# Reordered steps in two attentions, and another order of the opening in a feed-forward with ternary weights

## The chip, the cores and the metric

The kernel runs on one core of one Trainium2 chip. Its time is the device time of the program in microseconds (us). All times of the trace come from one profiled execution and count from its first instruction. The engines are PE (TensorE, matrix products; its weight loads, PEld, run beside it), DVE (VectorE), ACT (ScalarE), POOL (GpSimd) and SP (SyncE, which here only issues transfers). Each engine runs its own list of instructions in order; an instruction waits on semaphores that others raise.

## What is computed

Four layers follow each other on 16 blocks x[b] of 128 rows and 256 columns: L0 to L3, each an attention (L0a, L1a, L2a, L3a) and a feed-forward (L0f, L1f, L2f, L3f; L3f is itself an attention with weights mixed from experts). The change touches L1a, L1f and L3f:

```
# L1a: 16 heads of 16 columns; v's rows are dropped where the column sums of the probabilities are least
scores = softmax(q @ k.T / 4);  keep = int(S * 0.9)
mask = 1 for the `keep` keys with the largest scores.sum(over queries)
x = x + concat((scores * mask) @ v) @ Wo.T + bo
# L1f: two linear layers, weights rounded to -1, 0, 1, inputs to 8 bits
def bitlinear(x, w, b):
    x = x * rsqrt(mean(x * x) + 1e-5)
    s = 127 / max(abs(x), per row);  xq = round(x * s) / s
    return xq @ (round(w / mean(abs(w))) * mean(abs(w))).T + b
x = x + bitlinear(gelu(bitlinear(layernorm(x), w1, b1)), w2, b2)
# L3f: per block, Wq, Wk, Wv are a weighted sum of two of four experts
Wc = sum(weights[b, e] * W[e]);  x = x + softmax(q @ k.T / 4) @ v @ Wo + bo
```

## The kernel before

Everything stays on the chip: x_all holds the 16 blocks, each section (L1a, L1f, ...) is a stretch of its own with a barrier at either end, and each engine's list is written out by hand. An attention goes through the blocks one per turn (`step`). The names `cur`, `prev`, `nxt`, `new` stand for the block of the turn, the one before it and the next two; `last` is two blocks back in L1a (kind PRUNED) and one in L3f (kind MIXED). A block has its 16 heads in four quarters j of four heads.

In a turn PE computes the scores of `cur` (four banks S), turns the probabilities of each quarter (`turn_probs`, banks T[0] and T[1] in turn; a bank is free once the quarter two before was copied out), multiplies `last` with its values, turns the reciprocals of its row sums (`turn_recips`), projects k, q and v of `nxt` through one bank F, and `project_out`s `last`. ACT takes the exponentials (four instructions a quarter, line 900) and copies the turned reciprocals (rT, line 928); the turned quarters are copied out by ACT in L1a (line 548), by DVE and ACT in L3f (`mine`, lines 550 and 548). DVE takes the row minima (line 989), adds the biases of k, q and v (lines 1003, 1009, 1023), writes the normalised output oT (`norm_out`, line 1071) for which `project_out` (line 771) waits, and adds the result to x_all (`add_out`, line 1077). In L1a it also finds the keys to drop. In L3f ACT and DVE mix the weights of `new` in two parts each (`mixing.share`, `mixing.more`, lines 2562 and 2569); the first share waits for the v bias of a block two before.

L1f works on pairs of blocks, s = 0 and 1, in eight turns. Its opening turns the rounded weights on PE in ten lots (four of w1, two of the bias rows, four of w2; line 2015) and copies them to bf16 on ACT (line 1849). DVE aggregates the statistics (line 1902), POOL raises to the power -1/2 in two lots, of the first two blocks and of the other 14 (line 1727; once for the layer norm, once for the scale). For a pair DVE then normalises (xn, line 194), takes the row maxima (line 1928), the factor and the inverse (line 1942), ACT scales and rounds (xs, line 1882), PE turns it (line 2048) and ACT copies it out (xqT, line 1889). POOL splits the inverse in bf16 parts (lines 1816 to 1820), which PE turns (line 2032) for the bias product (line 2055) ahead of the w1 products (line 2057). ACT takes the GELU (line 1872), DVE its row maxima (line 1958) and rounds (hs, line 1981), PE turns it back (line 2025, banks T2), ACT and DVE copy (lines 1854 and 1962), PE multiplies with w2 (line 2039), DVE adds to x_all (line 1950), ACT sums squares (line 1862), and POOL adds the bias b2 (`add_b2`, line 1800). In a turn `old` is finished, `cur` is between the layers, `nxt` enters, and on DVE `far` is prepared. Turns 2 to 7 run in a counted loop.

Of the kernel before, what the change touches and what calls it, by code (L numbers as in the profile page):

```python
# [453 lines left out]
def attention(nc, g, name, kind, w, turned, needs, later=(), beside=None, after=None, out=None):  # L454
# [5 lines left out]
    with sec:  # L460
# [91 lines left out]
        with sec.block() as block:  # L552
# [96 lines left out]
            def _(pe):  # L649
# [141 lines left out]
                def step(st):  # L791
# [6 lines left out]
                    if pruned:  # L798
# [7 lines left out]
                        piece(nxt, project_k, new, prev)  # L806
                        piece(last, project_out)
                        piece(cur, turn_probs, 1)
# [81 lines left out]
            def _(act):  # L890
# [89 lines left out]
                if kind not in (MIXED, PLAIN):  # L980
                    load_table(act, g, ACT.Sqrt)

            @block.vector
            def _(dve):
# [102 lines left out]
                def step(st):  # L1087
# [43 lines left out]
                    else:  # L1131
# [28 lines left out]
                        mine(cur, 0)  # L1160
                        piece(last, norm_out)
# [569 lines left out]
def bitlinear_ffn(nc, g, w, q3, bias):  # L1731
# [4 lines left out]
    with sec:  # L1736
# [34 lines left out]
        flat = T2[0] + T2[1] + H[0] + H[1]  # L1771
# [9 lines left out]
        s_t_ps, s_t_sb = sec.sem("turned_ps"), sec.sem("turned_sb")  # L1781
        SPLIT = 5
        with sec.block() as block:
            @block.gpsimd
            def _(pool):
                pool.memset(a6[:, :], 0.0).then_inc(s_split, 1)
                for n, (lo, hi) in enumerate(((0, NS), (NS, NB))):
                    pool.wait_ge(ln.s_aggr, n + 1)
                    root_ln.pool(pool, g, ln.rstd[:, lo:hi, 0], base[:, lo:hi], ln.mv[:, lo:hi, 1], 1.0, LN_EPS, n + 1)
                    pool.wait_ge(s_ms, 2 * n + 2)  # L1790
                    if n == 0:
                        pool.wait_ge(root_ln.s, 1)
                    root_x.pool(pool, g, root[:, lo:hi], base[:, lo:hi], ms[:, lo:hi], 1.0, 1e-5, n + 1)
                pool.wait_ge(s_w2, 1)
# [40 lines left out]

                for n in range(TURNS + 2):
                    if n >= 2:
                        dequant(Pair(NS * (n - 2), n - 1))
                    if n < TURNS:
                        split(Pair(NS * n, n + 1))  # L1840
                        add_b2(Pair(NS * n, n + 1))

            @block.scalar
            def _(act):
                act.activation(warm[:, :], g.eps[:, :], ACT.Gelu)
                for k in range(len(lots)):
                    act.wait_ge(s_t_ps, k + 1)
                    sources, dst = lots[k]
                    act.copy(dst, flat[k % 8][:, :].bitcast(BF16)[:, 0:len(sources) * P]
                             .rearrange("p (m n) -> p m n", m=len(sources))).then_inc(s_t_sb, 1)  # L1850

                def turn_back(q, s, m):
                    act.wait_ge(s_qT_ps[1][s], q.v)
                    return act.activation(hqT[s][:, 4 * m:4 * m + 4, :],
                                          T2[s][m][:, :].rearrange("p (c t) -> p c t", c=4),
# [8 lines left out]
                def step(old, cur, nxt):  # L1864
# [1185 lines left out]
```

## Time and profile before

| | us |
|---|---|
| median of 3 runs | 1147.53 (1144.92 to 1149.98) |
| the profiled execution | 1141.54 |
| its span, first to last instruction | 1139.7 |

| engine | busy us | share of the span | instructions |
|---|---|---|---|
| PE | 1000.3 | 88% | 9262 |
| PEld | 815.5 | 72% | 9262 |
| DVE | 872.6 | 77% | 2482 |
| ACT | 724.1 | 64% | 2778 |
| POOL | 286.7 | 25% | 527 |

The mean granted clock of PE is 0.953 of full speed. The shares are means over sections with different limits, so the change has to be read section by section: L1a lies at about 240 to 420, L1f at 420 to 510 and L3f at 960 to 1140.

### The profile page before, as it was taken

The page shows a single profiled execution, that of the slowest core. Times are in us where ns is not written, and L with a number is a line of the kernel's source. Part 1 is how long each engine was busy: PE and PEld are TensorE (multiplying, and loading weights), DVE is VectorE, ACT ScalarE, POOL GpSimd, SP SyncE. Part 2 cuts the span into 40 slices and gives each one's busy share as a digit, 9 for nine tenths or more (in the row PEclk, how much of TensorE's full clock was granted, in tenths as well). Part 3 has the DMA queues.
Part 4 walks back from the last instruction along what each step waited for, and adds up shares of the span by engine and source line. Part 5 has one row for each costly group of instructions (what it writes and reads, how often), then busy time and mean ns, then how long its engine had stood idle before and what let it go on. Part 6 is the DMA issues. An engine that isn't in the chain of part 4 may idle for free. (4 is left out here: it accounts for less than half of the span.)

```text
span 1139.7 us, 27783 instructions
## 1 busy us (share of the span) xinstructions
PE 1000.3 (88%) x9262; PEld 815.5 (72%) x9262; DVE 872.6 (77%) x2482; ACT 724.1 (64%) x2778; POOL 286.7 (25%) x527
## 2 busy tenths in 40 slices
PE   6999967669999967878999979999997997889997
PEld 4888853247777843557777758999996986667775
DVE  5888989877888856975777755566655798689996
ACT  4887876768888866975777763112112544589995
POOL 4454530012222234422222210000000131333331
PEclk9999999679999997998999989999999998799999
DMA  9510000000000000005221000000000010000000
GB/s 282 133 30 1 3 1 1 0 15 16 15 12 11 11 2 1 0 6 130 85 82 52 10 2 1 0 0 0 0 1 19 24 29 6 5 12 14 14 14 20
DMA packets 43285, 30.17 MB, mean 26 GB/s; under 512 B 17208, under 2 KB 42432, under 8 KB 43200
## 3 DMA queue, kind: packets, MB, share of 16 engines
q1 hardware_dynamic: 43200, 29.10, 9.0%
q8 instruction: 46, 0.75, 0.3%
q14 instruction: 39, 0.32, 0.1%
HBM read 22.80 MB, written 2.10 MB: 22 GB/s over the span
## 5 line engine op out<-in xcount | busy, mean ns | idle before, releaser
L900 ACT ACTIVATE L1a_pr<-L1a_scores,L1a_nm 128x128 f32<-128x128 f32 x256 | 92.8, 415 | 4.5 <-DVE L1a_nm L989 3.8
L900 ACT ACTIVATE L2a_pr<-L2a_scores,L2a_nm 128x128 f32<-128x128 f32 x256 | 90.6, 390 | 6.0 <-DVE L2a_nm L989 6.0
L900 ACT ACTIVATE L0a_pr<-L0a_scores,L0a_nm 128x128 f32<-128x128 f32 x256 | 90.7, 395 | 4.4 <-DVE L0a_nm L989 4.4
L900 ACT ACTIVATION_READ_ACCUMULATOR L1a_pr<-L1a_scores,L1a_nm 128x1 f32 x256 | 65.1, 254 | 0.0
L989 DVE TENSOR_REDUCE L2a_nm<-L2a_scores 128x4 f32<-128x512 f32 x64 | 42.2, 683 | 24.9 <-PE L2a_scores L718 24.9
L2195 PE MATMUL L2f_inner<-L2f_taT,L2f_loraBT 128*128 128x128 f32 x512 | 59.7, 275 | 0.9 <-DVE L2f_hs L2347 0.9
L900 ACT ACTIVATION_READ_ACCUMULATOR L0a_pr<-L0a_scores,L0a_nm 128x1 f32 x256 | 60.1, 235 | 0.0
L2267 ACT COPY L2f_xTb<-L2f_xT 128x256 f32<-128x256 f32 x16 | 6.3, 411 | 84.5 <-PE L2f_inner L2184 84.5
L2184 PEld LDWEIGHTS L2f_inner<-L2f_xTb,L2f_wiT 128*128 128x128 f32 x512 | 58.3, 192 | 1.5 <-ACT L2f_loraBT L2151 1.2
L2184 PE MATMUL L2f_inner<-L2f_xTb,L2f_wiT 128*128 128x128 f32 x512 | 58.6, 275 | 0.9 <-ACT L2f_loraBT L2151 0.9
L2195 PEld LDWEIGHTS L2f_inner<-L2f_taT,L2f_loraBT 128*128 128x128 f32 x512 | 58.4, 192 | 1.1 <-issue 1.1
L900 ACT ACTIVATION_READ_ACCUMULATOR L2a_pr<-L2a_scores,L2a_nm 128x1 f32 x256 | 58.6, 229 | 0.0
L2208 PE MATMUL L2f_y_ps<-L2f_woT,L2f_hs 128*128 128x256 f32 x256 | 57.6, 379 | 0.0
L2208 PEld LDWEIGHTS L2f_y_ps<-L2f_woT,L2f_hs 128*128 128x128 f32 x256 | 47.6, 190 | 5.9
L2427 POOL MEMSET early_gates_spread_r<- 128x256 f32 x1 | 0.3, 312 | 198.2 <-POOLq L75 198.2
L900 ACT ACTIVATE L3f_pr<-L3a_logits_ps,L3f_nm 128x128 f32<-128x128 f32 x128 | 45.0, 382 | 3.6 <-DVE L3f_nm L989 3.6
L989 DVE TENSOR_REDUCE L1a_nm<-L1a_scores 128x4 f32<-128x512 f32 x64 | 41.0, 683 | 5.5 <-PE L1a_scores L718 5.1
L2562 ACT ACTIVATE mixing_mix<-experts,gates 128x1028 f32 (+1 forms) x32 | 33.5, 1046 | 18.1 <-DVE L3f_v L1023 14.1
L900 ACT ACTIVATE L3f_pr<-L3a_h_tilde,L3f_nm 128x128 f32<-128x128 f32 x128 | 44.8, 380 | 0.0
L671 PE MATMUL L3a_turned<-L3f_xT,mixing_mix 128*128 128x128 f32 x256 | 38.3, 296 | 7.3 <-ACT L3f_xT L907 6.8
L989 DVE TENSOR_REDUCE L0a_nm<-L0a_scores 128x4 f32<-128x512 f32 x64 | 42.0, 680 | 2.8 <-PE L0a_scores L718 2.8
L671 PEld LDWEIGHTS L3a_turned<-L3f_xT,mixing_mix 128*128 128x128 f32 x256 | 33.8, 205 | 11.8 <-ACT L3f_xT L907 10.3
(621 smaller groups left out, 3147.2 us busy)
## 6 DMA issues: line engine op xcount, KB each, us to landing
L_ffn_w_w<-in_L_ffn_w SPq DMA_DIRECT2D x2, 1024.0 KB, 6.8
L1a_ctxT<-ctxT_all SPq DMA_DIRECT2D x16, 128.0 KB, 2.0
L2a_ctxT<-ctxT_all SPq DMA_DIRECT2D x16, 128.0 KB, 2.0
L3a_mem<-in_ctx SPq DMA_DIRECT2D x16, 128.0 KB, 2.1
out<-x_all SPq DMA_DIRECT2D x16, 128.0 KB, 1.7
L0a_ctx_nat<-in_ctx SPq DMA_DIRECT2D x1, 1280.0 KB, 12.4
x_all<-in_x SPq DMA_DIRECT2D x1, 1024.0 KB, 9.4
L_ffn_wi<-in_L_ffn_wi SPq DMA_DIRECT2D x1, 1024.0 KB
```

The costliest lines, as they stand in the source:

```text
L671: mm = pe.matmul(F[:, m * P:m * P + P], W[:, c, m * P:m * P + P], inp[:, c, :], start=(c == 0), stop=(c == DC - 1))
L900: ex = act.activation(pr[q.s][:, j, h, :], S[j][:, h * P:h * P + P], ACT.Exp, bias=nm[q.s][:, j, h:h + 1], scale=-1.0, accum_out=ls[q.s][: ...
L989: dve.tensor_reduce(nm[q.s][:, j, :], S[j][:, :].rearrange("p (h k) -> p h k", h=2 * DC), AX.X, ALU.min).then_inc(s_mx[q.s], 1)
L2184: mm = pe.matmul(U[s][f // 4][:, f % 4 * P:f % 4 * P + P], wiT[:, c, f * P:f * P + P], xTb[s][:, c, :], start=(f % 4 == 0 and c == 0), sto ...
L2195: mm = pe.matmul(U[s][f // 4][:, f % 4 * P:f % 4 * P + P], bT[:, f * P:f * P + P], tb[s][:, k, :], start=False, stop=(k == 1), skip_group_ ...
L2208: mm = pe.matmul(Y[s][:, 0:D], hs[s][:, f, :], woT[:, f, :], start=(f == 0), stop=(f == FC - 1))
L2267: act.copy(xTb[s][:, :, :], xT[s][:, :, :]).then_inc(s_xTb[s], 1)
L2427: pool.memset(self.spread_r[:, :, :], 0.0).then_inc(self.s_set, 1)
L2562: act.activation(self.mix[q.s][:, lot], g.experts[:, first, lot], ACT.Copy, scale=g.gates[:, q.b, 0, :]).then_inc(self.s_share[n][q.s], 1)
```

## The change

Four edits. In L1a PE turns quarter 1 of `cur` ahead of `project_out` instead of behind it, and ACT's last instruction there loads the table of Gelu instead of that of Sqrt. In L3f DVE writes `norm_out` ahead of the copy of `cur`'s quarter 0. In L1f the opening has another order: the warm-up Gelu is gone; ACT copies w1 and the bias rows, scales the first pair, and only then copies two of the four w2 lots, while DVE copies the other two; POOL takes the powers of the 14 later blocks behind the first pair's split, and their second lot behind its add_b2; DVE aggregates those 14 behind the first pair's preparation. The banks of the lots follow from that (`turned_in`). Within the loop PE turns `nxt` between the two streams' second products instead of behind them. The last pair's turned h goes to the banks H, and its wait for the output of the pair before moves from the turning to the product.

```diff
@@ L1a, PE
                         piece(nxt, project_k, new, prev)
+                        piece(cur, turn_probs, 1)
                         piece(last, project_out)
-                        piece(cur, turn_probs, 1)
                         piece(nxt, project_q)
@@ attention, end of ACT's list
-                if kind not in (MIXED, PLAIN):
-                    load_table(act, g, ACT.Sqrt)
+                if kind in (PRUNED, MASKED):
+                    load_table(act, g, ACT.Gelu if pruned else ACT.Sqrt)
@@ L3f, DVE
-                        mine(cur, 0)
-                        piece(last, norm_out)
+                        if kind == MIXED:
+                            piece(last, norm_out)
+                            mine(cur, 0)
...
@@ L1f
-        flat = T2[0] + T2[1] + H[0] + H[1]
+        turned_in = T2[0] + T2[1] + [H[0][1], H[1][1]] + T2[0] + T2[1]
...
+        W1, B1 = range(4), range(4, 6)
+        W2_ACT, W2_DVE = range(6, 8), range(8, 10)
...
+        def turned(q):
+            return H if isinstance(q.v, int) and q.v == TURNS else T2
...
+                norm_roots(0, 0, NS)
+                scale_roots(0, 0, NS)
+                pool.wait_ge(s_w2, 1)
                 for n in range(TURNS + 2):
                     if n >= 2:
                         dequant(Pair(NS * (n - 2), n - 1))
                     if n < TURNS:
                         split(Pair(NS * n, n + 1))
+                        if n == 0:
+                            norm_roots(1, NS, NB)
                         add_b2(Pair(NS * n, n + 1))
+                        if n == 0:
+                            scale_roots(1, NS, NB)
@@ L1f, ACT
-                act.activation(warm[:, :], g.eps[:, :], ACT.Gelu)
-                for k in range(len(lots)):
...
+                take_weights(W1)
+                take_weights(B1)
...
+                    if nxt and not cur:
+                        take_weights(W2_ACT)
@@ L1f, DVE
                     if far:
+                        if nxt and not cur:
+                            mean_squares(1, NS, NB)
                         prepare(far, nxt)
                         if not nxt:
-                            mean_squares(1, NS, NB)
                             dve.wait_ge(root_x.s, 1)
                         if nxt and not cur:
                             dve.wait_ge(root_x.s, 2)
                         dequant(far, nxt)
+                        if not nxt:
+                            statistics(1, NS, NB)
+                            for k in W2_DVE:
+                                dve.wait_ge(s_t_ps, k + 1)
+                                dve.tensor_copy(*turned_lot(k)).then_inc(s_t_dve, 1)
...
-                statistics(1, NS, NB)
                 sweep_four(dve, step)
@@ L1f, PE
+                def turn_next(nxt, cur):
+                    for s in range(NS):
+                        pe.wait_ge(s_scaled[0][s], nxt.v)
...
                         for s in range(NS):
                             pe.wait_ge(s_scaled[1][s], old.v)
-                            pe.wait_ge(s_x[s], old.v)
+                            if turned(old) is T2:
+                                pe.wait_ge(s_x[s], old.v)
...
+                            if turned(old) is H:
+                                pe.wait_ge(s_x[s], old.v)
                             for f in range(FC):
                                 mm = pe.matmul(T2[s][0][:, 0:D], hqT[s][:, f, :], w2T[:, f, :], start=(f == 0),
                                                stop=(f == FC - 1))
                             mm.then_inc(s_y[s], 1)
+                            if s == 0 and nxt:
+                                turn_next(nxt, cur)
```

## Rows read from the trace of the kernel before

**Rows 1.** Windows of one turn: us, PE, PEld, DVE, ACT, POOL busy, clock, DMA share, GB/s.

```profile
320.25:330.27 10.02, 9.57 (x126) 7.92 (x125) 8.51 (x33) 8.27 (x38) 2.63 (x4) 1.00 0.04 13
...
440.84:451.77 10.93, 9.57 (x49) 5.68 (x50) 7.96 (x21) 8.03 (x16) 3.62 (x11) 0.75 0.01 2
...
478.19:487.11 8.92, 7.24 (x50) 4.89 (x50) 8.22 (x24) 8.15 (x16) 3.75 (x11) 1.00 0.00 0
```

**Rows 2.** Waits in L1a, 250 to 400: us in total, times, longest us.

```profile
PE L1a_values L771 <- DVE L1a_oT L1071: 5.4, 13, 0.5
```

**Rows 3.** Timeline of L1f's opening.

```profile
422.14 2.02 ACT L1849 COPY L1f_w1T<-L1f_h_turned 128x512 bf16<-128x512 bf16 x4
...
422.85 0.70 POOL L1727 TENSOR_TENSOR L1f_root<-L1f_base,minus_half 128x2 f32<-128x2 f32 x1
...
423.35 0.71 DVE L194 TENSOR_SCALAR L1f_xn<-x_all,L1f_ln_mv,L1f_ln_rstd 128x256 f32<-128x256 f32 x2
...
424.04 1.96 ACT L1849 COPY L1f_b1T<-L1f_hidden 128x1024 bf16<-128x1024 bf16 x2
...
427.31 2.58 POOL L1727 TENSOR_TENSOR L1f_root<-L1f_base,minus_half 128x14 f32<-128x14 f32 x1
...
427.75 1.18 ACT L1882 ACTIVATE L1f_xs<-L1f_xn,magic,L1f_factor 128x256 f32<-128x256 f32 x2
...
431.05 1.41 POOL L1800 TENSOR_TENSOR x_all<-x_all,L_ffn_b 128x256 f32<-128x256 f32 x2
...
431.25 0.26 PE L2032 MATMUL L1f_hidden<-identb,L1f_inverse_parts 128*128 128x128 bf16 x1 [7.60 <-POOL L1f_inverse_parts L1820]
...
431.69 1.24 DVE L194 TENSOR_SCALAR L1f_xn<-x_all,L1f_ln_mv,L1f_ln_rstd 128x256 f32<-128x256 f32 x2
...
432.59 0.58 PE L2055 MATMUL L1f_hidden<-L1f_b1T,L1f_inverse_rows 128*128 128x512 bf16 x1 [0.23 <-ACT L1f_xqT L1889]
...
434.23 0.16 DVE L1942 RECIPROCAL L1f_inverse<-L1f_dequant 128x2 f32<-128x2 f32 x1
...
436.65 1.22 DVE L1958 TENSOR_REDUCE L1f_am<-L1f_h 128x1 f32<-128x1024 f32 x1 [2.26 <-ACT L1f_h L1872]
```

**Rows 4.** Waits of DVE in L1f's loop, 452 to 497.

```profile
DVE L1f_am L1958 <- issue: 1.3, 4, 0.4
```

**Rows 5.** Timeline of a turn of L1a: start us, us, engine, line, what.

```profile
325.28 0.64 ACT L548 COPY L1a_prT<-L1a_probsT 128x512 f32<-128x512 f32 x1
...
326.23 1.13 PE L771 MATMUL L1a_values<-L1a_WoT,L1a_oT 128*128 128x256 f32 x4 [0.45 <-DVE L1a_oT L1071]
...
327.53 0.42 DVE L1077 TENSOR_TENSOR x_all<-L1a_values,x_all 128x256 f32 x1
...
327.64 1.06 PE L671 MATMUL L1a_projected<-L1a_xT,L1a_WqT 128*128 128x128 f32 x8
...
328.73 0.42 DVE L1009 TENSOR_TENSOR L1a_qT<-L1a_projected,L_xattn_bq 128x256 f32<-128x256 f32 x1 [0.19 <-PE L1a_projected L671]
```

**Rows 6.** Timeline of a turn of L1f's loop.

```profile
485.20 1.03 PE L2039 MATMUL L1f_h_turned<-L1f_w2T,L1f_hqT 128*128 128x256 bf16 x8 [0.60 <-DVE L1f_hqT L1962]
...
486.86 0.86 DVE L1950 SCALAR_TENSOR_TENSOR x_all<-L1f_h_turned,L1f_dequant,x_all 128x256 f32 x2
```

**Rows 7.** Timeline of L1f's last turn.

```profile
501.93 1.45 DVE L1981 TENSOR_SCALAR L1f_hs<-L1f_h,L1f_factor 128x1024 f32<-128x1024 f32 x2
...
503.92 1.94 PE L2025 MATMUL L1f_h_turned<-ident,L1f_hs 128*128 128x128 f32 x16 [1.01 <-DVE x_all L1950]
```

**Rows 8.** Waits of PE in L3f, 1010 to 1106.

```profile
PE L3a_turned L771 <- DVE L3f_oT L1071: 6.9, 10, 0.7
```

**Rows 9.** Timeline of a turn of L3f.

```profile
1056.90 1.03 PE L701 MATMUL L3a_turned<-mixing_mix,L3f_xT 128*128 128x256 f32 x4
...
1057.55 0.40 DVE L194 TENSOR_SCALAR L3f_xn<-x_all,kept_mv,kept_rstd 128x256 f32 x1
...
1057.97 0.42 DVE L1023 TENSOR_TENSOR L3f_v<-L3a_turned,mixing_mix 128x256 f32<-128x256 f32 x1
```

More of the change, by code:

```diff
@@ L1159, in step @@
                             late.vector_pooled(dve, T[1])
-                        mine(cur, 0)
-                        piece(last, norm_out)
+                        if kind == MIXED:
+                            piece(last, norm_out)
+                            mine(cur, 0)
+                        else:
+                            mine(cur, 0)
+                            piece(last, norm_out)
                         piece(nxt, add_q)
@@ L1961, in step @@
                         dve.wait_ge(s_qT_ps[1][1], old.v)
-                        dve.tensor_scalar(hqT[1][:, 4:8, :], T2[1][1][:, :].rearrange("p (c t) -> p c t", c=4),
+                        dve.tensor_scalar(hqT[1][:, 4:8, :], turned(old)[1][1][:, :].rearrange("p (c t) -> p c t", c=4),
                                           MAGIC, None, ALU.subtract).then_inc(s_qT2, 1)
@@ L2011, in _ @@
                         bias.wait(pe)
-                    if k >= 8:
-                        pe.wait_ge(s_t_sb, k - 7)
+                    if k >= 6:
+                        pe.wait_ge(s_t_sb, k - 5)
                     for m, src in enumerate(sources):
-                        mm = pe.transpose(flat[k % 8][:, :].bitcast(BF16)[:, m * P:m * P + P], src, g.identb[:, :])
+                        mm = pe.transpose(turned_in[k][:, :].bitcast(BF16)[:, m * P:m * P + P], src, g.identb[:, :])
                     mm.then_inc(s_t_ps, 1)
-                pe.wait_ge(s_t_sb, len(lots))
+                def turn_next(nxt, cur):
+                    for s in range(NS):
+                        pe.wait_ge(s_scaled[0][s], nxt.v)
+                        if cur:
+                            pe.wait_ge(s_gelu[s], cur.v)
+                        for c in range(DC):
+                            mm = pe.transpose(XT[s][:, c * P:c * P + P], xs[s][:, c * P:c * P + P], g.ident[:, :])
+                        mm.then_inc(s_qT_ps[0][s], 1)
                 def step(old, cur, nxt):
                     if old:
+                        if isinstance(old.v, int) and old.v == 1:
+                            pe.wait_ge(s_t_sb, W2_ACT[-1] + 1)
+                            pe.wait_ge(s_t_dve, len(W2_DVE))
                         for s in range(NS):
                             pe.wait_ge(s_scaled[1][s], old.v)
-                            pe.wait_ge(s_x[s], old.v)
+                            if turned(old) is T2:
+                                pe.wait_ge(s_x[s], old.v)
                             for f in range(FC):
-                                mm = pe.transpose(T2[s][f // 4][:, f % 4 * P:f % 4 * P + P],
+                                mm = pe.transpose(turned(old)[s][f // 4][:, f % 4 * P:f % 4 * P + P],
                                                   hs[s][:, f * P:f * P + P], g.ident[:, :])
                             mm.then_inc(s_qT_ps[1][s], 1)
+                    if nxt and not cur:
+                        turn_next(nxt, cur)
                     if nxt:
@@ L2031, in step @@
                             pe.wait_ge(s_gelu[0], cur.v)
+                        else:
+                            pe.wait_ge(s_t_sb, B1[-1] + 1)
                         pe.transpose(AT, a6[:, :], g.identb[:, :]).then_inc(s_aT_ps, 1)
@@ L2041, in step @@
                             mm.then_inc(s_y[s], 1)
+                            if s == 0 and nxt:
+                                turn_next(nxt, cur)
                     if nxt:
-                        for s in range(NS):
-                            pe.wait_ge(s_scaled[0][s], nxt.v)
-                            if cur:
-                                pe.wait_ge(s_gelu[s], cur.v)
-                            for c in range(DC):
-                                mm = pe.transpose(XT[s][:, c * P:c * P + P], xs[s][:, c * P:c * P + P], g.ident[:, :])
-                            mm.then_inc(s_qT_ps[0][s], 1)
+                        if cur and not old:
+                            turn_next(nxt, cur)
                         pe.wait_ge(s_aT, nxt.v)
```

23 lines of the change are left out of this document (13 added, 10 removed).

## The prediction

> **What bounds the kernel now.** I read the windows by turn first (where is an engine full?), then the waits of the engine that is full, then the timeline around each edited line, and asked there what ends last.
>
> In L1a a turn takes 10.02 us and PE is busy for 9.57 of it, DVE and ACT for under 8.6 [rows 1]: PE sets the pace, and the 0.45 it does not work is one wait, project_out for DVE's normalised output; it comes back in 13 turns with 5.4 us [rows 2]. With the first such turn, which lies outside that stretch's full turns, I count 14.
>
> In L1f two regimes follow each other. Its opening is a chain over four engines in which PE stands still for 7.60 us ahead of the first real work [rows 3]. From the third turn on the loop takes 8.92 us with DVE busy 8.22 and ACT 8.15 [rows 1]; DVE is the one that waits for nobody there (its only idle time before the big reduction is "issue", 1.3 us in four turns) [rows 4]. So the loop runs at DVE's pace, and what PE or ACT gains in it is worth nothing, but whatever the opening saves on DVE's clock is carried to the end. In L3f a turn is a ring through DVE, ACT and PE; DVE's last step of it, the v bias, starts right behind PE's v projection.
>
> **The change part by part.**
>
> *L1a, probabilities ahead of the output projection.* In the turn shown, project_out starts at 326.23 after a wait of 0.45, so PE was free at 325.78 [rows 5]. The step that now stands there, turn_probs(cur, 1), wants the exponentials of its quarter and a free T[1], which ACT's copy of the previous block's last quarter gives back at 325.28 + 0.64 = 325.92 [rows 5]. PE can go on at about 325.98, so 0.25 of the 0.45 is saved; project_out comes about 0.2 later than now. Nothing is added and no DMA moves: one queue (PE) is reordered, and the waits are those the two steps had. Who waits for project_out: DVE's add_out (327.53), behind which the statistics and the q bias are queued. A project_out that ends 0.1 to 0.2 later pushes add_out by about 0.08, since it now starts 0.17 after project_out's end. The q bias waits 0.19 for PE's project_q [rows 5], which comes 0.25 earlier; DVE's own queue allows at most those 0.19, less the 0.08. So 0.11 to 0.19 a turn; I take 0.13, times 14: **1.8 us**. Bounds: 0 (DVE's push eats it) and 14 x 0.19 = 2.7.
>
> *The table at L1a's end, and the warm-up.* The load at the end of L1a stays, of another table; L2a's is as before. L1f's opening loses a load and an activation ahead of ACT's first weight copy (422.14 [rows 3]). Worth about 1.0 on ACT (PE's first transposes bound it), counted in the next part.
>
> *L1f's opening, first pair.* Now: ACT copies ten lots, from 422.14 until xs begins at 427.75; POOL takes both long powers (14 columns, 2.58 us each) before it splits the first pair's inverse, so PE's turn of it is at 431.25 and the first hidden matmul at 432.59 [rows 3]. After: ACT has four lots (2.02) and two bias lots (1.96) before xs. From 422.14, xs is at 426.1; with the warm-up gone about 425.1. Then xs 1.18, two w2 copies (half of 2.02), and the xqT step: hidden matmuls at about 427.9, 4.7 earlier. POOL does not stand in the way any more: xn starts at about 422.5 (now 423.35, behind 14 aggregations), and from xn to the inverse the second pair took 431.69 to 434.39, of which 0.53 was xn being slow (1.24 against 0.71) [rows 3]; so the inverse is there at 422.5 + 2.2 = 424.7 and split, which now takes 429.89 to 431.25, is done at 426.1. The DVE takes two w2 copies here, an estimate of 0.6 each (half of a 1024-wide pass of 1.22 [rows 3]); they lie in time in which DVE has nothing else.
>
> *L1f's opening, second pair.* What was in front is now behind: the first long power runs 426.1 to about 429.0, add_b2 (1.41) to 430.4, the second long power to 433.3 (0.3 for the step ahead of each is an estimate). DVE's dequant of the second pair waits for it, and behind that wait in DVE's queue stands the big reduction of the first pair's GELU. So it starts at about 433.8, not at 436.65 [rows 3]: 2.9 earlier, although its input is ready before. Both reductions then run back to back (2 x 1.22), so the next hidden matmuls, now at 440.84 [rows 1], can start at about 436.8. I take **4.0 us**. Bounds: xn no earlier than now (0.85) and DVE slowed twice beside add_b2 (0.53 each) give 2.1; and that turn takes 10.93 us at a mean granted clock of 0.75 against 8.92 at 1.00 (2.4 GHz) [rows 1]; if PE keeps its high level, 2.0 more: 6.0.
>
> The Trainium skill (SBUF — State Buffer, section "SBUF: two separate sides") has the port pair of DVE and GpSimd as an exclusive lock for a whole instruction. The rows are divided: two xn passes took 0.71 although a power of 0.70 ran from 422.85, and 1.24 beside add_b2 [rows 3]. By the rule a 2.58 us power could shut out the second pair's xn; that result is a rival below.
>
> *L1f's loop.* PE now turns the next pair's x between the two streams' second matmuls. It is on no path while DVE is full [rows 1, 4]. What it could cost: the second stream's matmuls now also wait for ACT's xs. They start at 485.20 and take 1.03, and DVE fetches their result as the second half of a pass that begins at 486.86 (about 487.3) [rows 6], so there is 1.0 of room; the two turns take about 0.3. The waits written for the first old pair are not issued, as that pair lies inside the counted loop. **0**, bounds 0.1 a turn either way, six turns: 0.6 lost, 0.6 won.
>
> *L1f's last turn.* Its transposes go to the H banks and no longer wait for the previous pair's output: that wait is 1.01, until 503.92 [rows 7]. Their own input, hs, is half done at about 502.65 and whole at 503.38, so PE can start at 502.9. The chain behind (ACT's and DVE's copy back, the matmuls, the output) moves with it. **1.0 us**, bounds 0.5 and 1.0.
>
> *L3f, normalised output ahead of the copy.* DVE's order of a 0.41 and a 0.68 step is swapped, so their sum stays. PE's project_out waits 0.69 a turn for the first of them (6.9 in 10 turns) [rows 8] and gets it about 0.6 earlier; the copy is 0.4 later, and the transposes that need its bank come after project_out. PE's v projection thus ends up to 0.45 earlier. It ends at 1057.93 now, and DVE's v bias starts at 1057.97, though xn ahead of it ended at 1057.95 [rows 9] and DVE elsewhere starts a step 0.08 before the last one's end. So 0.10 a turn, 10 turns: **1.0 us**, bounds 0 and 2.0 (the turns at the edges).
>
> **The sum.** 1.8 + 4.0 + 1.0 + 1.0 = 7.8 us. Against the profiled execution (1141.54, of which the span is 1139.7) that is 1133.7. The median of the runs shown is 1147.53, 6.0 above that execution; I assume the same distance after: **1139.7 us**.
>
> **The rivals.**
> 1. *L1a's wait only changes its name.* If add_out's push or ACT's copy eats the gain, 1.8 falls away: 6.0 us, 1141.5. For it: the copy ends at 325.92, a third of the way from where PE came free to project_out's present start. Against: the q bias does wait for PE [rows 5]. Chance 0.13.
> 2. *POOL's long power shuts DVE out.* DVE's xn of the second pair meets the second power and waits it out: 2.6 lost, a sum of 5.2, 1142.3. For it: 1.24 beside add_b2. Against: 0.71 beside the short power [rows 3]. Chance 0.09.
> 3. *The change doesn't do what it says*: the opening's saving is given back at the first wait behind it, because DVE's 433.8 is what counts and the second turn then stalls on PE at low clock. Then 1 to 2 us remain of the opening, in all about 4: 1143.5. Chance 0.14.
> 4. *Slower: PE's clock.* The new opening strews PE's work thinly from 424 to 437. If the clock stays low into the loop, each turn costs 10.93 − 8.92 = 2.0 more [rows 1]. From four such turns on the gain is gone; with seven, 14.1 − 7.8 = 6.3 slower, 1153.8. Against: PE works 7.24 of 8.92 us in a loop turn at clock 1.00, and there the second turn brought it back. Chance 0.06.
>
> **How the numbers follow.** The forecast has 0.58. What this kernel's measurement can tell from no change is about 0.5%, 5.7 us. The forecast lies beyond that, and half of rival 1: faster 0.65. The other half, rivals 2 and 3 and half of rival 4 lie within: 0.32. Slower 0.03. The range: the parts' lower bounds sum to 2.0, the upper to 12.3, which is 1145.5 to 1135.2; the three runs lie 2.5 to either side of their median, and I add half of that: 1134 to 1146.7. It takes in rivals 1 to 3.
>
> **What would show it.** Right: in L1a no wait at project_out, a short one at turn_probs behind ACT's copy, and turns of about 9.9; in L1f the first hidden matmul 6.8 us behind ACT's first weight copy instead of 10.45 (422.14 to 432.59 [rows 3]), a DVE wait for POOL's power ahead of the first big reduction, loop turns still of 8.6 to 8.9, and no wait for x in the last turn; in L3f turns of 9.4. Wrong: L1a turns of 10.0 with DVE's q bias waiting for nobody; a slow xn beside the long power; loop turns above 9 us; a granted clock under 1.00 beyond the third turn.

## The result, and the profile after

| | us |
|---|---|
| before, median | 1147.53 (1144.92 to 1149.98) |
| after, median | 1138.76 (1137.76 to 1139.67) |
| ratio after / before, 95% interval | 0.9927 [0.9916, 0.9938] |
| after, profiled execution and its span | 1139.67, 1137.8 |

The kernel became faster by 8.4 us (7.1 to 9.6); 1139.7 was forecast. The total is right partly by luck: three terms of its sum are off (L1a 2.5 us too high, L1f's opening 0.9 and the order in its loop 1.0 too low), and they nearly cancel. Differences between kernels are taken from the ratios of their times to before's in the table, unless they are said to be by the medians. The profiled executions alone show 1.9 us (1139.67 against 1141.54), because that of before was a short one: its first normalised output of L1a stands at 275.75, while the thirteen other profiles here have it between 280.39 and 282.98, ahead of every edit. So the two traces are compared section by section, from a fixed instruction to a fixed instruction, not by their spans.

**L1a.** The wait groups of the steady turns of after (280.95 to 379.83: us in total, times, longest):

```profile
PE L1a_probsT L730 <- ACT L1a_prT L548: 2.5, 10, 0.3
...
DVE x_all L1077 <- PE L1a_values L771: 2.5, 9, 0.3
```

PE no longer waits for the normalised output (it was 0.4 a turn, [rows 2]) and now waits 0.25 for ACT's copy; add_out (L1077), pushed back, waits for PE; the wait of the q bias [rows 5] is gone. Ten turns take 98.88 us, against 99.96 of the same ten turns before: 9.89 instead of 10.00.

But the whole section did not gain. These are windows from the first normalised output of L1a to L1f's first aggregation, first of before, then of after (columns: us, busy time of PE, PEld, DVE, ACT, POOL with instructions, granted clock, DMA share, GB/s):

```profile
275.75:420.77 145.02, 131.96 (x1740) 108.15 (x1740) 116.42 (x468) 113.91 (x518) 37.62 (x62) 1.00 0.03 11
```

```profile
282.74:428.44 145.70, 133.50 (x1740) 108.20 (x1740) 116.83 (x468) 114.12 (x517) 37.66 (x62) 0.97 0.03 11
```

The same 1740 matmuls take longer at a mean clock of 0.97. The last two turns show where (windows of before, then of after, the end at L1f's first aggregation):

```profile
404.77:410.77 6.00, 4.40 (x79) 3.60 (x80) 3.37 (x18) 4.81 (x21) 1.66 (x2) 1.00 0.00 0
410.77:416.77 6.00, 3.54 (x45) 2.25 (x43) 3.46 (x20) 1.20 (x3) 2.44 (x8) 1.00 0.01 3
416.77:420.77 4.00, 1.13 (x4) 0.70 (x5) 1.27 (x4) 1.65 (x4) 0.04 (x1) 1.00 0.00 0
```

```profile
412.44:418.44 6.00, 4.04 (x78) 3.22 (x78) 3.84 (x22) 3.74 (x13) 3.38 (x7) 1.00 0.00 0
418.44:424.44 6.00, 3.90 (x40) 2.40 (x39) 2.01 (x8) 1.17 (x2) 0.72 (x4) 0.64 0.01 3
424.44:428.44 4.00, 1.77 (x4) 0.89 (x4) 0.85 (x3) 0.69 (x2) 0.04 (x1) 0.50 0.00 0
```

TensorE's granted clock falls to 0.50 (1.2 GHz) in after's last turn, where PE is busy for part of the time; before it stayed at 1.00 (2.4 GHz) to the end of the section, although PE was busy no more there (3.54 of 6 us in the second window). The last turn takes 6.06 us instead of 4.97, and from the last normalised output to L1f 4.79 instead of 3.84.

**L1f's opening** (timeline of after):

```profile
429.06 2.05 ACT L1871 COPY L1f_w1T<-L1f_h_turned 128x512 bf16<-128x512 bf16 x4 [3.93 <-PE L1f_h_turned L2045]
...
434.05 2.60 POOL L1731 TENSOR_TENSOR L1f_ln_rstd<-L1f_base,minus_half 128x14 f32<-128x14 f32 x1
...
435.81 0.59 PE L2102 MATMUL L1f_hidden<-L1f_w1T,L1f_xqT 128*128 128x512 bf16 x2 [1.15 <-ACT L1f_xqT L1914]
...
436.61 1.41 POOL L1815 TENSOR_TENSOR x_all<-x_all,L_ffn_b 128x256 f32<-128x256 f32 x2
436.68 0.68 DVE L1932 TENSOR_TENSOR L1f_ms<-L1f_ln_mv,L1f_ln_rstd 128x14 f32<-128x14 f32 x1 [1.76 <-POOL L1f_ln_rstd L1731]
...
438.52 2.61 POOL L1731 TENSOR_TENSOR L1f_root<-L1f_base,minus_half 128x14 f32<-128x14 f32 x1
...
441.17 0.22 DVE L1961 SCALAR_TENSOR_TENSOR L1f_dequant<-L1f_tmp,f_mean,L1f_root 128x2 f32<-128x2 f32 x1 [1.35 <-POOL L1f_root L1731]
...
441.51 2.33 DVE L1983 TENSOR_REDUCE L1f_am<-L1f_h 128x1 f32<-128x1024 f32 x2
...
444.40 0.58 PE L2100 MATMUL L1f_hidden<-L1f_b1T,L1f_inverse_rows 128*128 128x512 bf16 x1 [0.23 <-ACT L1f_xqT L1914]
```

The first hidden matmuls start 6.75 us behind ACT's first weight copy (predicted 6.8; the trace lacks the record of the very first, the bias product ahead of 435.81). DVE's dequant waits for POOL's second long power, and the two large reductions stand behind it, back to back. Counted from the section's first aggregation (420.77 before, 428.44 after), the first large reduction comes at 13.07 instead of 15.88 [rows 3] and the second pair's hidden matmuls at 15.96 instead of 20.07 [rows 1].

**L1f's last turn** (timeline of after):

```profile
500.24 2.52 DVE L1983 TENSOR_REDUCE L1f_am<-L1f_h 128x1 f32<-128x1024 f32 x2 [0.45 <-ACT L1f_h L1895]
...
503.67 1.45 DVE L2006 TENSOR_SCALAR L1f_hs<-L1f_h,L1f_factor 128x1024 f32<-128x1024 f32 x2
...
504.51 1.97 PE L2067 MATMUL L1f_hidden<-ident,L1f_hs 128*128 128x128 f32 x16
```

The transposes no longer wait for x [rows 7]. From the large reduction of the third pair, L1f before and after goes, from one large reduction to a later one: four turns 35.35 and 35.36; the step to the last pair's 7.78 and 6.76; from there to L2a's first aggregation 12.06 and 10.95.

**L3f.** Ten turns, from normalised output to normalised output, before and then after:

```profile
1017.01:1112.03 95.02, 86.19 (x920) 69.35 (x920) 87.94 (x161) 86.75 (x371) 36.57 (x41) 1.00 0.04 14
```

```profile
1015.94:1109.87 93.93, 88.60 (x923) 68.85 (x922) 87.19 (x161) 86.88 (x371) 36.58 (x41) 1.00 0.04 14
```

9.50 became 9.39. PE's wait for the output [rows 8] is gone from the list of its waits.

### The profile page after: what moved, and what is told of

Read it like the earlier page. It is cut to its first block and busy times, and to the rows that moved or that the text cites. A ratio compares the mean times of both kernels' runs of the same rounds, so it can differ in the third digit from the quotient of the medians.

```text
span 1137.8 us, 27771 instructions
## 1 busy us (share of the span) xinstructions
PE 1001.7 (88%) x9252; PEld 818.7 (72%) x9262; DVE 872.3 (77%) x2484; ACT 723.3 (64%) x2774; POOL 287.4 (25%) x527
## 5 line engine op out<-in xcount | busy, mean ns | idle before, releaser
L730 PE MATMUL L1a_probsT<-ident,L1a_pr 128*128 128x128 f32 x256 | 37.6, 280 | 7.5 <-ACT L1a_prT L548 5.6
```

The source lines that it names most:

```text
L730: mm = pe.transpose(T[j % 2][:, h * P:h * P + P], pr[q.s][:, j, h, :], g.ident[:, :])
```

## The experiments

Kernels of one number range shared a chip and their runs of before: 1 to 4 (before 1146.90), 5 to 8 (1146.85), 9 to 12 (1146.50).

The table gives, for each kernel, the median, the ratio to before with its interval, and from its one profile: the start of L1a's first normalised output; L1a from there to L1f's first aggregation; L1f to L2a's first aggregation; L2a to L3f's first maximum; and L3f's fill, from that maximum to L3f's first normalised output. Each is a difference of two starts of the trace. The profile is of one execution, the median of several, so a kernel's sections need not add up to its median. No edit touches the first and the fourth column; of the change itself, L1a's reorder is only in the second, and L3f's swap has its first turn at the end of the fifth.

| kernel | median | ratio | to L1a | L1a | L1f | L2a to L3f | fill |
|---|---|---|---|---|---|---|---|
| before | 1147.53 | | 275.8 | 145.0 | 89.8 | 462.6 | 20.4 |
| after | 1138.76 | 0.9927 [0.9916, 0.9938] | 282.7 | 145.7 | 82.8 | 464.0 | 16.9 |
| 1 L1a alone | 1147.29 | 0.9998 [0.9981, 1.0015] | 282.9 | 145.7 | 90.1 | 463.7 | 17.5 |
| 2 L3f alone | 1145.36 | 0.9988 [0.9975, 1.0000] | 281.2 | 145.1 | 90.3 | 463.7 | 16.9 |
| 3 L1f alone | 1140.52 | 0.9941 [0.9916, 0.9965] | 282.7 | 145.1 | 83.1 | 462.6 | 18.6 |
| 4 order undone | 1143.20 | 0.9974 [0.9962, 0.9987] | 280.9 | 144.5 | 83.7 | 466.0 | 19.6 |
| 5 after again | 1138.54 | 0.9926 [0.9912, 0.9939] | 283.0 | 145.7 | 82.7 | 463.8 | 17.0 |
| 6 tail filled | 1135.12 | 0.9899 [0.9884, 0.9914] | 280.4 | 144.5 | 83.3 | 461.2 | 16.9 |
| 7 powers cut up | 1140.45 | 0.9945 [0.9931, 0.9958] | 280.4 | 145.7 | 81.5 | 464.7 | 19.5 |
| 8 banks undone | 1138.26 | 0.9923 [0.9910, 0.9937] | 282.1 | 145.7 | 83.9 | 462.7 | 17.0 |
| 9 before, tail filled | 1147.04 | 1.0001 [0.9990, 1.0012] | 282.1 | 145.1 | 90.4 | 463.9 | 17.5 |
| 10 L1a alone, tail filled | 1141.27 | 0.9961 [0.9942, 0.9981] | 281.8 | 143.6 | 86.8 | 464.7 | 20.3 |
| 11 after, tail filled less | 1137.14 | 0.9911 [0.9888, 0.9934] | 282.2 | 143.6 | 82.2 | 462.7 | 19.7 |
| 12 combined | 1134.86 | 0.9907 [0.9885, 0.9929] | 281.3 | 143.6 | 81.6 | 463.5 | 17.0 |

**1 to 3. Each part alone.** Theory, after the two traces: L1f gives 7.0 us, L3f 1.1, L1a 1.5.

```diff
                         piece(nxt, project_k, new, prev)
+                        piece(cur, turn_probs, 1)
                         piece(last, project_out)
-                        piece(cur, turn_probs, 1)
```

> The kernel before with the L1a reorder alone. Theory: the trace after shows 9.89 us a turn of L1a against 10.00, and the last quarter of the reorder's work on PE still waits 0.25 a turn for ACT's copy; 14 turns by 0.11 give 1.5 us, so 1.5 us faster than before, turns of 9.89, DVE's q bias waiting for nobody and DVE's add_out waiting about 0.28 for project_out. Rival: the shorter turns come from the state in which the rest of the changed kernel leaves the engines, and the wait only changes its name here: turns of 10.0 and no difference in time.

L1a alone is worth nothing (0.2 us faster, 1.7 slower to 2.2 faster). Its turns are 9.89, as the theory wanted; its section is 145.7 instead of 145.0, and the timeline of its last two turns shows the same low clock that after has: the last output projection at

```profile
424.32 2.07 PE L771 MATMUL L1a_values<-L1a_WoT,L1a_oT 128*128 128x256 f32 x4 [0.92 <-DVE L1a_oT L1071]
```

where before and all turns ahead of it have 1.13 [rows 5]. Theory and rival both miss: the wait did not only change its name, and yet nothing is left.

```diff
-                        mine(cur, 0)
-                        piece(last, norm_out)
+                        if kind == MIXED:
+                            piece(last, norm_out)
+                            mine(cur, 0)
...
```

> The kernel before with the L3f swap alone. Theory: turns of 9.39 instead of 9.50 us, 10 turns, 1.1 us faster than before; the 2.9 us that the profiled execution of the changed kernel gained in the fill of L3f ahead of its first normalised output is TensorE's granted clock (0.50 there in before, 1.00 in after) and not this edit, so the fill is as often long as short. Rival: the swap gives the fill's 2.9 us as well, and the kernel is 4.0 us faster.

1.4 us faster (0 to 2.9), turns of 9.40: as the theory says. The rival's 4.0 is out. The fill was 16.9 here, but 17.5 in experiment 9, which does not have the swap, and 19.6 in experiment 4, which has it: most of the 3.5 between the traces of before and after goes with the clock and not with this edit. A smaller part is the edit's. Where the clock is low for 1.3 to 1.6 us of the fill, it takes 16.9 to 17.0 with the swap (after, 2, 5, 6, 8, 12) and 17.5 without (1, 9); where it is low for 8.6 to 9.0 us, 19.5 to 19.7 with it (4, 7, 11) and 20.3 to 20.4 without (before, 10). From L3f's first maximum to the end of the program the swap is worth about 1.4: 162.6 us here, 164.0 and 164.2 in experiments 1 and 9, and with the longer fill 165.1 to 165.2 with it (4, 7, 11), 166.5 to 166.6 without (before, 10).

```diff
+                W1, B1 = range(4), range(4, 6)
...
+                    if nxt and not cur:
+                        take_weights(W2_ACT)
...
+                            if s == 0 and nxt:
+                                turn_next(nxt, cur)
```

> The kernel before with all the edits of L1f alone (opening, order of TensorE's work in the loop, banks of the last turn, the Gelu table loaded at the end of L1a). Theory, from the two traces: 4.9 us up to the third pair's large reductions, 0 in the loop's turns, 2.1 from the last turn of the loop to L2a's first aggregate, together 7.0 us faster than before. As predicted it would be 5.0 (4.0 and 1.0). Rival: half of the opening's 4.9 is the clock that this one execution happened to get, and the kernel is 4.5 us faster or less.

6.8 us faster (4.0 to 9.6); the interval holds the theory's 7.0, the predicted 5.0 and the rival's 4.5. In the profiles the section takes 83.1, against 89.8 to 90.4 in four of those with the old L1f (before, 1, 2, 9), which is the theory's 7.0. The rival comes back with the fifth, experiment 10, below: part of the opening's gain does hang on the clock.

**4. TensorE's order in L1f's loop undone.**

```diff
                             mm.then_inc(s_y[s], 1)
-                            if s == 0 and nxt:
-                                turn_next(nxt, cur)
                     if nxt:
-                        if cur and not old:
+                        if cur:
                             turn_next(nxt, cur)
```

> The changed kernel with TensorE's order in L1f's loop put back: the turning of the next pair's inputs behind both products and not between them. As predicted: the loop is held by DVE, so no difference from the changed kernel, turns of 8.9. Theory now: no difference in the turns, but 1.0 us lost where DVE is not the bound, in the last pair's large reduction (a wait of 1.5 for ACT's h instead of 0.45), and up to 0.8 in the first turn, so 1.0 to 1.8 us slower than the changed kernel, 7.0 to 7.8 us faster than before.

In L1f it is as the theory now said: turns of 8.92, and the last pair's large reduction waits again:

```profile
498.11 2.51 DVE L1983 TENSOR_REDUCE L1f_am<-L1f_h 128x1 f32<-128x1024 f32 x2 [1.47 <-ACT L1f_h L1895]
```

1.02 more than after's 0.45; the step to it is 7.79 (after 6.76, before 7.78), all else in L1f is after's, and the section is 0.9 longer. The prediction's "0" for the order held for the turns and failed in the last one. The whole kernel, though, lost more than any theory gave: 3.0 us faster than before where after (experiment 5, on another chip) is 8.5, so 5.5 slower than after, or 4.7 by the two medians. The two profiled executions are only 2.3 apart, and what is longer there, besides L1f's 0.9, lies in code that this edit does not touch: L2a to L3f took 466.0 instead of 464.0, and L3f's fill 19.6 instead of 16.9, at another clock. Five-microsecond windows from L3f's first maximum on, of after and then of this kernel:

```profile
975.18:980.18 5.00, 3.65 (x32) 2.35 (x32) 3.59 (x7) 4.37 (x21) 2.57 (x8) 0.86 0.01 3
980.18:985.18 5.00, 3.65 (x28) 3.28 (x28) 3.93 (x8) 2.43 (x14) 1.52 (x1) 1.00 0.00 0
985.18:990.18 5.00, 4.05 (x63) 3.14 (x62) 3.80 (x9) 4.16 (x17) 1.10 (x2) 1.00 0.00 0
```

```profile
975.09:980.09 5.00, 3.97 (x32) 2.43 (x32) 3.28 (x7) 4.37 (x21) 2.24 (x7) 0.80 0.02 3
980.09:985.09 5.00, 3.34 (x16) 3.34 (x17) 2.69 (x7) 2.42 (x14) 1.84 (x2) 0.54 0.00 0
985.09:990.09 5.00, 4.95 (x36) 3.91 (x34) 3.30 (x7) 1.44 (x3) 0.00 (x0) 0.78 0.00 0
```

In the second window PE gets 28 matmuls done at 1.00 and 16 at 0.54. So the time of a kernel contains, besides the edit's own microseconds, where the clock falls behind it; 1 us of an edit can't be read from it.

**5 to 8.** Theory by now: L1f 7.0, L3f 1.0, L1a nothing net, because of the clock in its last turns.

> The changed kernel as it is, beside the three that follow. Theory: L1f gives 7.0 us, L3f 1.0, L1a nothing net (1.5 in its turns, given back in its last turns, where TensorE is granted 0.50 instead of 1.00), so 8.0 us faster than before. Rival: L1a's turns count in full and the kernel is 9.5 us faster.

The changed kernel as it is: 8.5 us (7.0 to 10.1) faster. Both sums lie in the interval; experiment 1 has told them apart.

```diff
+                    def keep_busy(n):
+                        if not cur and last:
+                            for _ in range(n):
+                                pe.transpose(S[0][:, 0:P], g.ident[:, :], g.ident[:, :])
...
+                        keep_busy(6)
                         piece(last, project_out)
```

> The changed kernel with 26 transposes of the identity, which nobody reads, put on TensorE in the last two turns of L1a, in front of the waits for the normalised output, the kept scores and the values, and at the end. Theory: TensorE idles in these turns, its granted clock falls to 0.50 there, and that costs 1.1 us in the last turn (6.06 against 4.97) and 0.95 in the last output projection (2.07 against 1.13); with the idle time filled the clock stays at 1.00 and the kernel is up to 2.0 us faster than the changed one. Rival: the fall of the clock has nothing to do with what TensorE does in these turns, it falls at the same place and the kernel is the same or 0.5 us slower for the added work. Third: the fall only moves into L1f's opening, where the hidden matmuls then take 1.06 instead of 0.59 for two, and the total is the same.

(The transposes were 36, not 26.) The clock was 1.00 through these turns, the last turn 4.97 again, and L1a 144.5 instead of 145.7; the twelve at the end ran past the wait that they were to fill and took 0.8 of the gain. The theory's mechanism is there, and the rival (the clock does not heed what PE does) is out. The third came true in a small part: the clock is low again in L1f's opening while the first two pairs' hidden matmuls run, and L1f takes 83.3 instead of 82.7. The kernel is 3.4 us faster than after on the same chip by the medians, of which L1a is 1.2; the rest is in sections that the edit does not touch, above all L2a to L3f (461.2 against 463.8).

```diff
-                            norm_roots(1, NS, NB)
-                        add_b2(Pair(NS * n, n + 1))
+                            norm_roots(1, NS, 2 * NS)
+                            scale_roots(1, NS, 2 * NS)
+                            norm_roots(2, 2 * NS, NB)
...
+                            scale_roots(2, 2 * NS, NB)
+                            add_b2(Pair(0, 1))
```

> The changed kernel with POOL's two long powers in L1f's opening cut up: the second pair's two columns first, the other twelve columns later, the bias of b2 behind them. Theory: in the trace after, the second pair's chain is held by POOL's two powers of 14 columns (2.60 and 2.61 us) and by the two products of 14 columns on DVE beside POOL's bias addition (0.68 and 0.65); two columns take 0.73, so the second pair's inverse comes about 2 us earlier, its first hidden matmul starts 14.0 us behind L1f's first aggregate instead of 15.96, and the kernel is 2.0 us faster than the changed one. Rival: ACT, which works without a pause from 437.1 to 441.9, is the next bound, and at most 0.5 us comes back.

POOL was the bound, as the theory says: the second pair's hidden matmuls start at 439.86, 13.7 behind the first aggregation (15.96 in after). The rival's 0.5 is out, but only 1.2 of the 2.2 reach the loop. 0.7 go because DVE's next steps meet POOL's bias additions, now two pairs in a row, so that DVE comes to the second pair's first large reduction 1.5 earlier than in after and no more:

```profile
439.91 1.90 DVE L2010 TENSOR_SCALAR L1f_hs<-L1f_h,L1f_factor 128x1024 f32<-128x1024 f32 x2
...
440.54 3.32 POOL L1815 TENSOR_TENSOR x_all<-x_all,L_ffn_b 128x256 f32<-128x256 f32 x4
...
441.74 1.54 DVE L194 TENSOR_SCALAR L1f_xn<-x_all,L1f_ln_mv,L1f_ln_rstd 128x256 f32<-128x256 f32 x2
```

(1.45 and 0.72 elsewhere.) The rest goes in the second reduction, which waits 0.61 for ACT's h, whose hidden matmuls ran at the low clock (1.06 us for two; 0.59 at 1.00). And the kernel as a whole is 1.9 us slower than after by the medians: L2a to L3f 464.7, fill 19.5.

```diff
-            return H if isinstance(q.v, int) and q.v == TURNS else T2
+            return T2
```

> The changed kernel with the last pair's large transposes put back into the PSUM banks of the turns before (so that they wait for the output of the pair ahead). As predicted: the wait of 1.0 for x comes back in the last turn and the kernel is 1.0 us slower than the changed one. Rival: DVE, which has to add the outputs of the pair ahead and then of the last pair, is the bound there, and nothing changes.

The wait is back, and nothing hides it:

```profile
505.04 1.94 PE L2067 MATMUL L1f_h_turned<-ident,L1f_hs 128*128 128x128 f32 x16 [1.02 <-DVE x_all L1975]
```

From the last large reduction to L2a 12.07 us, against 10.95: 1.1 (1.0 was predicted). The rival is out. The median shows no difference (0.3 faster), with L2a to L3f 1.1 shorter.

**9 to 12. Is L1a's gain real where the clock stays?** The same idle time filled with 24 transposes (the expectations miscount them as 18), in the kernel before, in the kernel with L1a's reorder alone, and in the changed one.

```diff
+                        if not prev:
+                            keep_busy(4)
                         piece(last, values)
...
+                        keep_busy(4)
                         piece(prev, turn_kept)
```

> The kernel before with transposes of the identity, which nobody reads, on TensorE in the idle time of L1a's last two turns (18 of them, none behind the last output projection but four). Theory: before's L1a tail already runs at the granted clock of 1.00 in its profile, so L1a's own time (first normalised output to L1f's first aggregate, 145.0) doesn't change; the fall of the clock that came in L1f's opening may move. Same time as before, within 2 us. Rival: the transposes lift the clock in what follows by themselves, and the kernel is 3 us faster, as the changed kernel with them was.

> The kernel before with L1a's reorder and the same transposes in L1a's last two turns. Theory: the reorder's 1.5 us in the turns (9.89 against 10.00) is no longer given back in the last turns (4.97 and 3.84 instead of 6.06 and 4.79), so first normalised output to L1f's first aggregate is 143.6 instead of 145.0 to 145.7, and the kernel is 1.5 us faster than the one with the transposes alone. Rival: the reorder costs as much elsewhere as it saves in the turns, and the two kernels with transposes take the same time.

Without the reorder L1a takes 145.1 and the kernel its old time: filling idle time is no gain by itself. With it L1a takes 143.6: the 1.4 us of the turns, kept (143.65 against 145.06 ahead of rounding). The whole kernel is 4.6 us faster than experiment 9 (5.8 by the medians; its nine runs lie between 1138.75 and 1147.57), more than the theory's 1.5. The two profiled executions are 2.2 apart: L1a is 1.4 shorter, L1f 3.6, though its code is the old one in both, and L2a to L3f with the fill 3.5 longer. The windows from L1f's first aggregation to the third pair's large reduction, of before, of experiment 10, of after and of experiment 11, in this order:

```profile
420.77:455.38 34.61, 22.74 (x141) 13.41 (x142) 21.01 (x82) 25.37 (x47) 17.32 (x40) 0.75 0.00 1
```

```profile
425.46:457.03 31.57, 18.89 (x139) 12.48 (x142) 21.01 (x82) 25.40 (x47) 17.37 (x40) 0.89 0.00 1
```

```profile
428.44:458.12 29.68, 22.37 (x141) 15.07 (x144) 22.54 (x83) 23.50 (x43) 17.70 (x40) 0.79 0.00 1
```

```profile
425.89:454.99 29.10, 19.47 (x141) 12.55 (x144) 22.33 (x83) 23.40 (x43) 17.68 (x40) 0.94 0.00 1
```

The old opening takes 34.6 us at a mean clock of 0.75 and 31.6 at 0.89, the new one 29.7 at 0.79 and 29.1 at 0.94. So of the 4.9 us that the opening gained, 2.5 are left between these two profiles with a high clock (0.89 and 0.94, not the same); the rest is that the new opening suffers less from a low one.

> The changed kernel with 18 such transposes in L1a's last two turns, without the twelve behind the last output projection that ended 0.8 us later than the wait there. Theory: L1a 143.6 us from its first normalised output to L1f's first aggregate (144.5 with the twelve, 145.7 without any), 2.1 us less than the changed kernel, and 0.8 less than with the twelve. Rival: the clock falls again in the last output projection as soon as TensorE idles behind it, and 144.5 stays.

L1a 143.6: the theory's number, the rival's 144.5 is out. The last two turns, in windows that end at L1f's first aggregation like those of after above, are at 1.00 throughout:

```profile
409.89:415.89 6.00, 4.33 (x79) 3.50 (x80) 3.35 (x18) 4.82 (x21) 1.66 (x2) 1.00 0.00 0
415.89:421.89 6.00, 5.36 (x64) 4.32 (x63) 3.46 (x20) 1.21 (x3) 2.44 (x8) 1.00 0.01 3
421.89:425.89 4.00, 1.93 (x12) 1.34 (x11) 1.27 (x5) 1.60 (x3) 0.04 (x1) 1.00 0.00 0
```

The kernel's gain over after (1.4 by the two medians, of different chips) is not resolved, and the 0.8 over experiment 6 did not show: by the medians it is 2.0 slower, with L2a to L3f and the fill 4.3 longer in the profile.

```diff
                             late.tensor_turn(pe, T[1])
+                            for _ in range(10):
+                                pe.transpose(T[0][:, D:D + P], g.ident[:, :], g.ident[:, :])
                             pe.wait_ge(late.by_vector, late.POOLED)
```

> The changed kernel with the 18 transposes in L1a's last two turns, POOL's long powers cut up as before, and 10 more unread transposes in front of TensorE's wait of 2.7 us in the fill of L3f. Theory: L1f 81.5 us as with the powers cut up alone; L3f's fill (first maximum to first normalised output) 17.0, as it is at the granted clock of 1.00, and not 19.5, as it was with the powers cut up alone: 1.2 us faster than the changed kernel with the transposes alone. Rival: what is saved in L1f shifts where the clock falls in L2f to L3f, as with the powers cut up alone (4.6 us there), and the kernel is 2 us slower than the changed one with the transposes.

L1f 81.6 and the fill 17.0, both as expected. Against experiment 11 it is 0.5 us faster (2.3 by the medians), with intervals that overlap, so the theory's 1.2 and the rival are not told apart. It is 10.7 us faster than before (11.6 by the medians), not separable from experiment 6 (11.6 and 11.7). That the ten transposes made the fill short isn't shown: it was 16.9 without them in experiment 6 and 19.7 in 11. Experiments 6 and 12 have the lowest medians here.

## Why the prediction was right, point by point

| part | predicted | in the traces |
|---|---|---|
| L1a | 1.8 | 1.4 in the turns, 2.05 lost at the end: −0.7 in all |
| L1f's opening | 4.0 | 4.9 |
| L1f's loop order | 0 | 0 in the turns, 1.0 in the last step |
| L1f's last turn | 1.0 | 1.1 |
| L3f | 1.0 | 1.1 in ten turns |
| sum | 7.8 | 7.4 (whole kernel: 8.4, 7.1 to 9.6) |

Some 1 us between the sum and the whole is not attributed: it is within the interval, and the stretches that no edit touches moved by more.

*L1a* is the step that failed, in its result though not in its mechanism. The turn moved by 0.11, of the predicted 0.13, with each wait where the prediction put it: ACT's copy ahead of the transposes, add_out pushed back, the q bias served. What it left out is the end of the section. It priced the turns and left out the last two, where PE is busy for 3.54 of 6 us. In the trace of before their clock is 1.00, so the loss could not be read there; but a falling clock was a rival for L1f only, not for L1a. The fall of the clock took 1.1 back in the last turn and 0.95 behind it (0.95 alone in experiment 4, whose L1a is 144.5). Rival 1's number (nothing from L1a) came true by a mechanism that no rival named. That PE's idle time has a part in the fall is shown: 6, 10, 11 and 12 keep 1.00 to the end of the section, and against 1 and after the transposes are all that 10 and 11 add. Why it comes earlier with the reorder, in all six profiles that have it without filling (after, 1, 4, 5, 7, 8) and in none of the four that lack it (before, 2, 3, and with the filling 9), isn't settled: the waits of PE ahead of it are much alike with and without it (the longest 1.42 us in after and 1.29 in before, the others within 0.05 of each other).

*The opening.* As far as the prediction followed it, it came out to 0.1: the large reduction 2.8 earlier (2.9), the next hidden matmuls 4.1 earlier (4.0), and DVE waiting for POOL's second power, with the reductions behind it back to back. The 0.8 that it lacks came after that: the second pair's two large reductions began 2.55 us apart before and 1.52 after, since TensorE's clock rose again while that pair's hidden matmuls ran. The bound "if PE keeps its high level, 2.0 more" looked at the new opening alone, which gains 0.6 from a high clock (experiment 11); the old one gains 3.0 (experiment 10), so where both have it the change is worth less, not more. The edits of the opening were not run one by one: how the 4.9 splits among them is read from the trace, not shown.

*The loop order.* "0, DVE is full" was right for the four turns (35.35 and 35.36) and wrong for the last, which has no pair further ahead: DVE's normalisation and reduction of it (0.72 and 0.73 for the pair) fall away there, DVE comes early and waits for GELU, and GELU for PE. There PE's earlier start is worth its full 1.0.

*L1f's last turn* and *L3f* are right, in place and size; for L3f the prediction counted ten turns, and the turns at the edges, which it had in its bounds, bring it to about 1.4 (experiment 2).

*The base.* To take the sum from the median, not from the profiled execution, was right. "The same distance after" was not: the profiled execution of before lay 6.0 below its median, that of after lies 0.9 above. The forecast did not need it, as the 7.8 came off the median either way.

*The rivals.* DVE's xn of the second pair hardly met POOL's power (0.72 for the pair at 437.97, with the power from 438.52), so the opening alone doesn't test that rival. Where they do meet, the power did not shut DVE out: two xn that began inside a power of 0.88 in the loop took 0.40 each (from 473.27 on in after), and in experiment 7 the first hs, 1.6 us into a power of 2.42, took 0.75 (the pair's usual 1.45 is two such). But POOL's bias addition did hold DVE: the two products for ms took 0.68 and 0.65 beside it, 0.17 each before, and ended within 0.1 of its two halves. The Trainium skill (SBUF — State Buffer, section "SBUF: two separate sides") describes this as an exclusive lock for a whole instruction, for a DVE instruction with two SBUF inputs among others; the trace agrees for the products, and experiment 7 with it for hs and xn. It does not agree for the powers, which are also GpSimd instructions, and there the measurement decides. The slower rival (a clock that stays low into the loop) did not come: 1.00 from 447.5 us on, while the second pair was in its turn, and loop turns of 8.6 to 8.9 from the third pair on.

## What to carry to other kernels

Below a per cent, compare a change section by section between fixed instructions of the trace, with the granted clock beside each, and take several profiles: here the medians hid an edit worth 1.1 us (experiment 8), and whole-kernel times made one of 1.0 look like 5 (experiment 4). The last turn of a pipelined loop lacks the work that makes one engine the bound; price it on its own. A saving in front of a stretch where TensorE is busy only part of the time can be lost to its clock there; unread transposes in its waits kept the clock up, and they cost nothing only while they end before the wait does.

## What the runs showed of the hardware

TensorE's clock fell to 0.50 at 420.2 us of after, behind a stretch in which no idle time of PE was longer than 1.42 us (until 411.10), but where it was busy for only 4.04 of 6 us. In the same place of before it was busy for 4.40 and then 3.54 of 6 us, with pauses of up to 1.29, and kept 1.00: what decides between the two is not shown. Transposes that nobody reads, put into these pauses, kept it at 1.00 in four kernels of four.

Where the clock falls differs from profile to profile: the stretch from L2a to L3f, whose code is the same in all, took 461.2 to 466.0 us, and L3f's fill 16.9 to 20.4. In the one kernel with two profiles (after and 5, on two chips) the falls lie in the same places, within 0.3 us. But the runs of before spread from 1141.35 to 1150.01, so a kernel need not always get the same, and with one profile of each other kernel it isn't shown what belongs to a kernel and what to an execution. So edits of 1 us can't be added up from whole-kernel times. In the steps that they touch they can be read: undone, the order and the banks gave back the 1.0 and the 1.1 that they had brought (experiments 4 and 8).
